# Reciprocals of a head's sums spread by DMAs through DRAM, sums over heads in four column strips, first convolution part in quarters

## What is computed

```python
q = elu(x @ wq.T + bq) + 1;  k = elu(x @ wk.T + bk) + 1;  v = x @ wv.T + bv
kv_cos = einsum('bshx,bshz->bhxz', k * cos, v)          # and kv_sin
qkv = einsum('bshx,bhxz->bshz', q * cos, kv_cos) + einsum(..., q * sin, kv_sin)
denom = 1.0 / (q_cos . sum(k_cos) + q_sin . sum(k_sin) + 1e-05)  
t = t + (qkv * denom[..., None]).reshape(b, s, h * d) @ dense_w.T + dense_b
```

## Time and profile before

| | us |
|---|---|
| median of 3 runs (lowest, highest) | 3843.64 (3842.21, 3851.14) |
| the profiled execution | 3844.39 |
| its span, first to last instruction | 3842.6 |

### The profile page before, as it was taken

The page is one execution under the profiler, slowest core; times in us unless marked ns, Lnnn a source line. Parts: engine busy times, 40 slices in busy tenths (PEclk is TensorE's granted clock), DMA queues, the critical chain, the costliest instruction groups (busy, mean ns, idle before and its releaser), DMA issues.

```text
span 3842.6 us, 52421 instructions
## 1 busy us (share of the span) xinstructions
PE 3480.2 (91%) x17588; PEld 1723.1 (45%) x17588; DVE 2928.1 (76%) x3293; ACT 1710.6 (45%) x1808; POOL 1777.5 (46%) x1638
## 2 busy tenths in 40 slices
PE   3799998999999998999989999999989999999976
PEld 2444444444543445444544445434444445444453
DVE  6887877878688877878778786888778786758823
ACT  0166524754256533665246542565336552443210
POOL 1067721866148741677228761487317771211200
PEclk8899999999999999999999999999999999999967
DMA  1000000000000001000000000000010000100045
GB/s 50 18 1 1 1 17 27 1 1 1 22 23 1 1 1 44 1 1 1 18 27 1 1 1 26 18 1 1 1 44 1 1 1 18 31 1 1 1 123 212
DMA packets 18670, 70.92 MB, mean 18 GB/s; under 512 B 8781, under 2 KB 13421, under 8 KB 13485
## 3 DMA queue, kind: packets, MB, share of 16 engines
q1 hardware_dynamic: 18365, 67.10, 5.6%
HBM read 37.26 MB, written 29.84 MB: 17 GB/s over the span
## 4 chain that ended last, share of the span: by engine, by line
PE 48%; issue 21%; POOL 15%; DVE 11%; ACT 3%; DMA 1%; SPq 1%; POOLq 0%; DVEq 0%; ACTq 0%
PE ps_D L1554 16%; POOL arena L570 9%; POOL UA L580 4%; PE ps_E L1518 4%; PE ps_C L1543 4%; PE ps_B L1501 4%; PE ps_A L1501 3%; PE ps_D L1325 2%; DVE arena L939 2%; PE ps_E L1529 2%; PE ps_B L1305 2%; PE ps_A L1305 1%; PE ps_C L1472 1%; PE ps_E L1567 1%; DVE ST L986 1%
## 5 line engine op out<-in xcount | busy, mean ns | idle before, releaser
L570 POOL TENSOR_TENSOR arena<-arena,UHL 128x896 f32<-128x896 f32 x525 | 1087.6, 2089 | 168.0 <-ACT UHL L722 149.2
L1554 PE MATMUL ps_D<-region,small 128*128 128x448 f32 x1792 | 768.3, 552 | 22.8 <-DVE OS L1149 22.6
L1122 DVE TENSOR_TENSOR region<-region,ps_C 128x896 f32<-128x896 f32 x448 | 485.9, 1085 | 279.8 <-PE ps_C L1543 279.2
L722 ACT ACTIVATE UHL<-arena,W8C 128x896 f32<-128x896 f32 x525 | 541.9, 1032 | 0.0
L1554 PEld LDWEIGHTS ps_D<-region,small 128*128 128x128 f32 x1792 | 316.9, 191 | 324.1 <-issue 285.3
L758 ACT ACTIVATE EQ<-ps_B,NEG 128x896 f32<-128x896 f32 x224 | 225.7, 1008 | 476.2 <-PE ps_B L1501 476.2
L580 POOL TENSOR_TENSOR UA<-region,CS 128x128 f32<-128x128 f32 (+1 forms) x400 | 229.3, 575 | 408.1 <-PE ps_C L1472 358.9
L1472 PE MATMUL ps_C<-region,UA 128*128 128x512 f32 (+1 forms) x800 | 378.4, 595 | 2.9 <-ACT region L656 2.8
L758 ACT ACTIVATE EQ<-ps_A,NEG 128x896 f32<-128x896 f32 x224 | 225.5, 1007 | 339.4 <-PE ps_A L1501 339.4
L939 DVE SCALAR_TENSOR_TENSOR arena<-arena,W8C 128x448 f32<-128x448 f32 (+1 forms) x243 | 364.9, 1523 | 0.0
L1089 DVE SCALAR_TENSOR_TENSOR region<-region,ps_A 128x1024 f32<-128x1024 f32 (+1 forms) x200 | 242.2, 1211 | 100.0 <-ACT region L740 98.2
(11 more groups left out here) (299 smaller groups left out, 5824.1 us busy)
## 6 DMA issues: line engine op xcount, KB each, us to landing
arena<-x SPq DMA_DIRECT2D x8, 1568.0 KB, 7.1
t_keep<-Y SPq DMA_DIRECT2D x7, 1568.0 KB, 7.2
w_keep<-region SPq DMA_DIRECT2D x7, 784.0 KB, 5.6
CST<-t_keep SPq DMA_DIRECT2D x2, 1568.0 KB, 9.8
small<-t_keep SPq DMA_DIRECT2D x2, 1568.0 KB, 12.3
plane<-w_keep SPq DMA_DIRECT2D x4, 784.0 KB, 16.1
UHL<-t_keep SPq DMA_DIRECT2D x2, 1568.0 KB, 12.6
out<-CST SPq DMA_DIRECT2D x2, 1568.0 KB, 12.1
```

Source lines behind the costliest of these rows:

```text
L570: pool.tensor_tensor(out=X[:, cut], in0=X[:, cut], in1=PRODUCT[m % 3], op=ALU.add).then_inc(pool_taps.sem, 1)
L722: act.activation(PRODUCT[m % 3].rearrange("p (h w) -> p h w", w=W), g_window(2 * g * ROWS + 2 * (k // 5), 2 * (k % 5) - 4, 2 * ROWS), ACT. ...
L1122: dve.tensor_tensor(out=q, in0=q, op=ALU.mult, in1=here.area(key)[:, :].rearrange("p (c n) -> p c n", c=2)[:, :, 0:PIX])\
L1554: ins = pe.matmul(here.area(key)[:, 0:PIX], MW[i][:, c, :], Q[s % 3][:, c, :], start=c == 0, stop=c == NCHUNK - 1)
```

## The change

Five edits:

1. The reciprocals of a step are stored to a DRAM tensor `r_keep` by four DMAs (one for each strip of 112 tokens, 16 rows of 448 bytes each) and read back by four DMAs of 64 partitions x 4 rows x 448 values, in which all 64 partitions read the same row, into a new SBUF tile `RB`: two for quarters 0 and 1 (h = 0), two for quarters 2 and 3 (h = 1). All eight are issued by SyncE. GpSimd's `split` and TensorE's `q_broadcast` are gone. RB has one buffer: the loads of half h for step s wait until step s - 1 has been scaled from it (`scaled`).
2. `q_scale` reads RB in SBUF in place of PSUM area C. Its lag is 10 slots in place of 8; the outputs, their sums, the folds and the normalisation come two slots later, and the stage has 70 slots in place of 68. The outputs alternate between areas D and C; the fold moves from E to C.
3. `q_sums` writes four column strips of 32 rows and 112 columns, so the 1e-5 and the reciprocal work on 128 x 112 in place of 96 x 224.
4. The first convolution part works in quarters of 64 x 64, for two chunks at a time (four groups, in slots 57, 59, 61 and 63); ScalarE evicts each group in four instructions of 64 partitions, in place of two of 128.
5. The logits of two chunks go to the two halves of one area, four groups in place of seven.

The hunks stand in the order of the file: constants, tiles, SyncE, VectorE (`q_scale`, `den_reciprocal`), TensorE (`front`, `q_sums`, logits).

```diff
-SUB = PIX // 2
+SUB = PIX // 4
-DEN_LAG, SUM_LAG, RECIP_LAG, RB_LAG, OUT_LAG, PARTS_LAG, FOLD_LAG = 4, 5, 6, 8, 9, 13, 18
+DEN_LAG, SUM_LAG, RECIP_LAG, RB_LAG, OUT_LAG, PARTS_LAG, FOLD_LAG = 4, 5, 6, 10, 11, 15, 20
-FRONT_SLOTS = {SLOTS + 1 + n: n for n in range(NPIX)}
-LN2_SLOTS = {27: 0, 43: 1, 59: 2, 67: 3}
-ALL_SLOTS = 68
+FRONT_SLOTS = {SLOTS + s: g for g, s in enumerate((1, 3, 5, 7))}
+LN2_SLOTS = {29: 0, 45: 1, 61: 2, 69: 3}
+ALL_SLOTS = 70
...
-        RR = sb("RR", [96, 3, SUB])
-        RS3 = sb("RS3", [96, 2, SUB], BF16)
+        RB = sb("RB", [P, 4, 2 * PIX])
+        RR = sb("RR", [P, 2, SUB])
...
+                for s in range(STEPS):
+                    sp.wait_ge(*recip_ready.at(pair, s + 1))
+                    passed(sp)
+                    for q in range(STRIPS):
+                        sp.dma_start(r_keep[HEADS * (s % 2):HEADS * (s % 2 + 1), q * SUB:(q + 1) * SUB],
+                                     RR[q * STRIP:q * STRIP + HEADS, 1]).then_inc(recip_stored.sem, 16)
+                    sp.wait_ge(*recip_stored.at(pair, s + 1))
+                    passed(sp)
+                    for h in range(2):
+                        if s >= 1:
+                            sp.wait_ge(*scaled.at(pair, 4 * (s - 1) + 2 * h + 2))
+                            passed(sp)
+                        for i in range(2):
+                            at = HEADS * (s % 2) + 8 * h + i
+                            sp.dma_start(RB[HALVES[i], 2 * h:2 * h + 2, :].rearrange("p b (c n) -> p (b c) n", n=PIX),
+                                         bass.AP(r_keep.tensor, r_keep.offset + at * PIX,
+                                                 [[0, C], [2 * PIX, 4], [1, PIX]]))\
+                                .then_inc(spread_loaded[h].sem, 16)
...
             def q_scale(here, s, cc):
-                key = ("rb", s, cc)
                 q = Q[s % 3][:, 2 * cc:2 * cc + 2, :]
-                dve.wait_ge(*here.filled(key))
+                dve.wait_ge(*spread_loaded[cc // 2].at(here.pair, s + 1))
                 dve.tensor_tensor(out=q, in0=q, op=ALU.mult,
-                                  in1=here.area(key)[:, :].rearrange("p (c n) -> p c n", c=2)[:, :, 0:PIX])\
-                    .then_inc(*here.empty(key))
+                                  in1=RB[:, cc].rearrange("p (c n) -> p c n", c=2)).then_inc(scaled.sem, 1)
...
             def den_reciprocal(here, s):
                 dve.wait_ge(*here.emptied(("dsum", s)))
                 if s >= 1:
-                    dve.wait_ge(*split_ready.at(here.pair, s))
+                    dve.wait_ge(*recip_stored.at(here.pair, s))
                 dve.reciprocal(RR[:, 1], RR[:, 0]).then_inc(recip_ready.sem, 1)
...
                     for k in range(3):
-                        ins = pe.matmul(here.area(key)[:, 0:PIX], W2T[:, k, :],
-                                        g_window(4 + n * ROWS, k - 1, ROWS), start=k == 0, stop=k == 2)
+                        for b, row in enumerate(parts):
+                            for i in range(2):
+                                ins = pe.matmul(here.area(key)[HALVES[i ^ b], i * 512:i * 512 + rows * W],
+                                                W2T[HALVES[i], k, HALVES[i]],
+                                                g_window(4 + row, k - 1, rows)[HALVES[i]],
+                                                start=k == 0, stop=k == 2)
...
-                for j in range(2):
-                    ins = pe.matmul(here.area(key)[0:96, 0:SUB],
-                                    SEL[:, j].rearrange("p m d h -> p (m d h)"),
-                                    DS[:, j * SUB:(j + 1) * SUB], start=j == 0, stop=j == 1)
+                for q in range(STRIPS):
+                    ins = pe.matmul(here.area(key)[q * STRIP:(q + 1) * STRIP, 0:SUB], SEL[:, :],
+                                    DS[:, q * SUB:(q + 1) * SUB], start=True, stop=True)
...
-                for n in range(NPIX):
-                    key = ("lg", n)
+                for g in range(NG):
+                    key = ("lg", g)
                     pe.wait_ge(*here.room(key))
-                    pe.matmul(here.area(key)[0:C, 0:PIX], GWT[:, :], U2[:, n * PIX:(n + 1) * PIX],
-                              start=True, stop=True).then_inc(*here.fill(key))
+                    for n in range(2 * g, min(2 * g + 2, NPIX)):
+                        ins = pe.matmul(here.area(key)[HALVES[n % 2], 0:PIX], GWT[:, :],
+                                        U2[:, n * PIX:(n + 1) * PIX], start=True, stop=True)
+                    ins.then_inc(*here.fill(key))
```

123 lines of the change are left out of this document (43 added, 80 removed).

## The result

The median went from 3847.39 us (3842.21 to 3853.42, 4 runs) to 3809.16 us (3805.87 to 3813.36, 4 runs): 0.9904 of the time before, 95% interval 0.9885 to 0.9924. I had forecast 3677 us, 4.4% less; 1.0% came. The sign held, and the time lies in the wide range of 3600 to 3920, but above the 3590 to 3785 us that the forecast gave its own case, and the size is a quarter of what was forecast. Lines of the changed kernel that matter: 1104 features, 1112 scaling, 1132 reciprocal, 1138 output products, 1512 denominators, 1533 outputs, 467 stores, 477 spreading loads, 587 GpSimd's tap additions, 930 VectorE's taps.

The account below looks back on a forecast made before the run. TensorE was taken to bound the query stage at 14.0 us a step. Savings of 7 x (13.2 + 7.5 + 1) = 152, last pair 10 and setup 5, together 167, from 3844.4 gave 3677 us; range 3600 to 3920.

Parts of the forecast that it names:

- TensorE's share: Query stage step: without broadcasts (1.6 us) and with shorter head sums (0.35 us saved), TensorE's 14.0 us fall to 12.1.
- The DMA chain: Query stage: reciprocal to landing of the spreading loads, L, takes 9.8 us (8.1 to 11.8), so a step takes at least 12.2.
- An ordinary step: Query stage step without normalisation: from 14.0 to 12.7 us (12.1 to 13.7), 1.3 us saved.
- three bounds in series: Query stage step: bounds of 12.1 (TensorE), 12.2 (VectorE with GpSimd) and 12.2 us (DMAs) together give 12.7 us.
- The wait of a scaling for GpSimd: Query stage: VectorE's other work lies mostly beside GpSimd's additions, leaving about 0.5 us of waiting for a scaling.
- 9.5 ordinary steps and two of normalisation ... two save 0.8: Query loop, slots 10 to 56: ordinary steps save 12.4 us, two normalisation steps 0.8, in all 13.2 us a pair.
- The end: Slot 56 to the last residual: 38.3 us falls to 28.3, set by the DMAs; 7.5 of the 10 saved is kept.
- Logits and setup: Logits save 1 us a pair; twelve setup instructions become one, saving 5 us.
- The fast bound: Whole kernel: 12.1 us a step, normalisation at 1.4 saved, 10 at the end, 255 us in all, 3590 us.
- a chain of L = 10.8 to 11.7: Reciprocal to landing of the loads takes 10.8 to 11.7 us, which still leaves 3785 to 3830 us; chance 0.08.
- The locked engines: Rival: each query-stage scaling waits 1.04 us for a GpSimd addition, 14.5 us a step, 3844 us; chance 0.10.
- The slow chain: Rival: the scaling waits for the first two spreading loads, the DMAs set the step, 3950 us at L = 13; chance 0.22.

Follow-up runs that it names:

- no_chain: Changed kernel without the eight DMAs of each step; the scaling reads a buffer set once to 1.0 and waits for no DMA: 3739 us, ratio 0.9723.
- small_sums: Changed kernel with GpSimd's additions of the query stage cut from 896 columns to 8: 3701 us, ratio 0.9624.
- filler: Changed kernel with four TensorE passes that nobody reads added in the slot of the 4.22 us gap, twice a pair: 3771 us, ratio 0.9811.
- late_taps: Changed kernel with VectorE's convolution taps moved from the query stage's last eight slots to after the last normalisation: 3767 us, ratio 0.9797.
- the runs of 3: First convolution part whole again in the changed kernel (3833 us, 0.9958), and in quarters, alone, in the kernel before (3818 us, 0.9918).
- halves: Changed kernel with each GpSimd tap addition of 896 columns issued as two of 448, in the key stage too: 3809 us, 0.9914.
- whole_front: Changed kernel with the first convolution part whole again, seven chunks of three passes of the whole array: 3833 us, ratio 0.9958.
- four small edits: Changed kernel with reciprocal before scaling, taps out of the last eight slots, TensorE filling passes, GpSimd additions halved in the query stage only: 3704 us, 0.9622.

## Why the prediction was right and where it was wrong

- **TensorE's share: near.** The broadcasts are gone and the eight head sums take 0.40 us as shown, 0.33 from start to start (0.40 forecast). The loop of a pair lost 18.7 us of TensorE's work (162.4 to 143.7), where 1.95 us a step makes 22.4 for its 11.5 steps; the 143.7 hold passes at 1.2 GHz.
- **The DMA chain: right in its terms.** Four stores take 1.7 us to issue (1.4), land after 2.1 us (1.9); loads land after 6.2 us (6.3). From the end of the reciprocal (962.03) to the scaling (972.21) it is 10.2 us; the shortest of all steps is 9.9, the median 10.8. Forecast: L = 9.8. The broadcast load that the forecast leans on has packets of 1,792 bytes in the trace, not rows of 256; that speaks for it all the more, since the spreading loads have rows of that size too. The two slots of lag cost nothing at the start (21.0 and 21.1 us), as forecast.
- **An ordinary step: right in its length, not in what it saves.** 12.80 us in the rows, 12.85 in the mean of the first three, against 12.7; the fourth, between the normalisations, takes 13.7. The reciprocal takes 0.84 us (0.8). But the chain is not one of three bounds in series: without any DMA (no_chain) the second and third steps take 12.8 us all the same. And 14.0 us was the wrong base. The window that I read has three steps in 41.46 us, 13.8 each, and the four ordinary steps of the loop have a mean of 13.7 before and 13.1 after: 0.7 us saved in each, not 1.3.
- **The wait of a scaling for GpSimd: near.** 0.5 us forecast; the excess over 1085 ns is 18.7 us a pair, 0.33 for each of 56.
- **The step that failed first: "9.5 ordinary steps and two of normalisation ... two save 0.8".** Only four of the ten steps in the loop are ordinary. From output product to output product the loop reads, before, 13.5, 14.5, 13.5, then 18.4, 15.7, 14.6, then 13.5, then 18.4, 15.0, 14.5; after, 13.0, 12.8, 12.8, then 15.9, 17.7, 14.8, then 13.7, then 15.9, 16.2, 12.7 (means of seven pairs). The ordinary ones saved 2.7 us together, where the forecast has 12.4. What hid this from me is that 9.5 x 14.0 + 2 x 18.4 is 169.8 us, the length of the loop: the count fits by chance. Each normalisation reaches over three steps, and the six of them saved 3.4: the first of three gains 2.5 us, the second loses 2.0 and 1.2. Without GpSimd's additions the same six take 81.5 us in place of 93.2 (small_sums: 13.9, 13.9, 13.0, 13.8, 14.2, 12.7). I had priced the lock for the scaling of an ordinary step, where other work lies beside an addition; in the step of normalisation shown above VectorE waits twice (1.78 and 2.42 us) and TensorE waits for it (4.22), and I had written "gains 0.7 of waiting". In the sum this term stands with 13.2 us a pair and measured 6.0; with the additions narrowed to 8 columns it measured 20.6 (171.1 to 150.5).
- **Behind it, TensorE's clock.** Nothing in the forecast had it. The stage was TensorE's alone (41.46 of 41.46 us), and its clock at 1.00 over the whole loop of the pair shown (2.4 us at 1.2 GHz in the mean of seven pairs). Freed of 18.7 us of work it has gaps, and behind the long ones it runs at 1.2 GHz, 17.1 us in the mean. filler shows 4.7 us a pair for it. I took a shorter TensorE queue for a gain that could at worst be hidden; here some of it is taken back.
- **The end: wrong by three terms.** The quarters gave 5.1 to 5.4 us, not the 7.7 of TensorE's work. The other edits lengthened the same stretch by 4.1, and the way behind it by 2.3. I had named the DMA chain as what sets the end, at 28.3 us from slot 56 to the last residual; it is 37.9 (951.05 to 988.97). Its three legs: to the first scaling of step 12 it is 9.1 us (6 forecast), from there to that of step 13 12.0 (12.2), and behind it 16.8 (10.1). The last is longer because behind the chain's last wait VectorE's queue isn't empty: taps and parts of a normalisation stand between the scalings. late_taps shows 4.1 us of that. I had laid the chain, TensorE's order and VectorE's queue beside each other, where the first and the last are in series.
- **Logits and setup.** From the first pass of the logits to the first of the convolution behind them it is 5.4 us (7.0 before): 1.5 saved (1 forecast). But that convolution then takes 2.2 us longer from first pass to last (27.2 to 29.5), so the pair doesn't keep it. The setup saved 10.3, not 5, since I had left out that it has the quartered part as well (4.8 to 5.3 us in the runs of 3). The last pair and what lies behind it saved 4.0, not 10. There GpSimd has no additions, and the loop gives 11.8 us (165.4 to 153.6), near the 13.2 forecast; but the end costs 9.4 (22.6 to 32.0), and that is the DMA chain: no_chain has 22.2 there.
- **The sum.** The fast bound has 22.8 us a pair where its parts give 9.5 x 1.9 + 2.8 + 1 = 21.9; that moves it from 3590 to 3596 us and changes nothing. The measured time falls into the 3785 to 3830 us that a chain of L = 10.8 to 11.7 was given (0.08). That is luck: in the pairs of the loop all of the chain is worth 5.4 us.
- **The rivals.** "The locked engines" had the right mechanism, but by its price each scaling would have waited 1.04 us and the kernel come out at 3844; a third of that wait, in the right place, was enough to take most of the loop's gain. "The slow chain" (0.22) was wrong in the loop.

The Trainium skill (SBUF - State Buffer, section SBUF: two separate sides) calls the pair of ports that VectorE and GpSimd share an exclusive lock, not a bandwidth split, held for the whole instruction. The rows agree for single operations (854.64, 858.18). What follows for shorter instructions isn't what one would read into it: with halves the mean excess of a scaling falls by a quarter, from 290 to 224 ns over 1085, not by half, and a scaling can wait for several in a row (2561.49).

The 2.3 us behind the last output product are TensorE's clock again. Windows from that product to the next correlation, first and second pair, columns as above:

```profile
545.24:556.78 11.54, 8.44 (x45) 7.13 (x46) 7.86 (x12) 5.23 (x7) 4.86 (x3) 0.70 0.33 139
986.52:995.34 8.82, 5.64 (x45) 4.73 (x46) 7.95 (x12) 5.01 (x7) 2.52 (x1) 1.00 0.43 182
```

The same 45 passes take 11.5 us where the clock is at 0.70 in the mean and 8.8 where it is at 1.00 (8.5 in every pair before). Five of the seven pairs have 6.8 us at 1.2 GHz there, two have none: 4.9 us in the mean, none before. TensorE has waited several times for 0.6 to 2.0 us ahead of it, in both kinds of pair. whole_front has 3.9 us at 1.2 GHz there (10.6 us long), filler 2.4 (9.9), late_taps none (8.9). So about 2.0 of the 2.3 us are the clock, and late_taps' gain behind the stage is that too.

What stays open: what about the quarters makes the stretch from correlation to features longer (with them it has 17.1 us at 1.2 GHz, and 14.6 in whole_front); the last 17 us of GpSimd's additions; why halves of them make the key stage longer; and what the two slots of lag alone do in the kernel before, which wasn't measured.

## What to carry to other kernels

When the engine that sets a stage is relieved, write down each step of the stage with what VectorE has in it, not an ordinary step times a count: here the ordinary steps gained 2.7 us, not 12.4, and those with a normalisation lost to GpSimd what they could have gained. An operand moved from PSUM to SBUF costs nothing in its own duration (1.08 us either way), and here it cost 63 us through GpSimd. If such a change brings little, look at the order of the work before giving it up: with four small edits on top the change is worth 3.8% in place of 1.0%.

## What the runs showed of the hardware that was not expected

The lock holds small operations with a single SBUF operand as well, but not reductions. Durations of line 978 in the kernel after (128x14, min/median/max ns); then, in the kernel before, three additions of GpSimd in a row, and a reduction and the same small operation of VectorE that run beside them:

```profile
L978 DVE TENSOR_SCALAR ST<-ST x64: 172/174/1795, 152.1 to 3621.9; 128x14 f32<-128x14 f32 x48, 128x8 f32<-128x8 f32 x16
```

```profile
861.29 6.18 POOL L570 TENSOR_TENSOR arena<-arena,UHL 128x896 f32<-128x896 f32 x3 [0.34 <-ACT UHL L722]
```

```profile
864.94 1.08 DVE L986 TENSOR_REDUCE ST<-un 128x14 f32<-128x896 f32 x1
866.05 1.46 DVE L987 TENSOR_SCALAR ST<-ST 128x14 f32<-128x14 f32 x1
```

The small operation takes 172 ns alone and up to 1795 beside an addition, and 1.46 us here, where it ends with the third addition (867.51 and 867.47). The reduction of 896 columns lies whole beside the additions and takes 1.08 us, its time alone, and they take 2.06 each. The spreading loads, 129 GB/s over the loop, landed after 6.2 us in the median (4.6 to 9.6). A run of GpSimd's instructions back to back can keep a VectorE operation waiting through all of them: 5.70 us for a scaling of 1.08, behind five halves. And about 50 us of useless passes on TensorE (16 x 3.17) made the kernel 36 us faster, because the stretches at 1.2 GHz behind two gaps of 4.2 us a pair went.
